# Score maxima by causal blocks of 32 queries and 4 heads, put into the query tile by DMA, and attention's steps in a new order

## The chip, the cores and the metric

The kernel runs on one core of a Trainium2 chip. The metric is the device time of one execution in microseconds (us). All times below are of that one core.

## What is computed

Two transformer-like layers on x of 16 x 256 x 128 (4096 tokens). Layer 0 has a modulated layer norm, causal attention, then a mixture of 8 experts (top 2) with a shared expert. Layer 1 is a gated recurrence with two gated products. The change is in the attention of layer 0, whose core is this (16 heads of 8 dimensions, 4 key heads, n = 256):

```python
q5 = q.reshape(b, reps, KV_HEADS, n, D_HEAD)
scores = jnp.einsum('brknd,bkmd->brknm', q5, k) / scale
causal = jnp.tril(jnp.ones((n, n), dtype=bool))
scores = jnp.where(causal, scores, jnp.float32(-jnp.inf))
p = jax.nn.softmax(scores, axis=-1)
s = jnp.einsum('brknm,bkmd->brknd', p, v)
```

## The kernel before

**Planning.** Python code plans the whole kernel ahead. `schedule()` makes jobs, each a short list of steps (a step has a name and a key such as the batch), and `arrange()` merges the jobs in the order that the string `ORDER1` spells (two characters pick the job whose next step comes) up to the first experts' tiles, and `ORDER2` for layer 1. The table `HELD` (how long a step holds its engine), `LANDS` and `BEHIND` (how long until its result can be used) serve only to choose PSUM banks and to place `fill` products, which keep TensorE active. Each engine then runs its own steps strictly in that order. A step waits on semaphores for what it needs.

**Stages.** First x is turned, normalised and modulated in chunks c of 512 tokens (8 chunks of 2 batches). Attention runs over 16 batches b, interleaved with the norms of later chunks and with the routing of earlier ones. After the last batch (`woh` 15, which writes X at L1400) SyncE fetches expert weights (`fetch`, `load_late`), the experts' tiles run, and then layer 1. From `woh` 15 on, memory of attention is used again, so nothing of the fetches can start sooner.

**Attention of one batch.** `spm`/`spe` (L977, L1808) put the queries of a chunk into QS, four groups g of 128 rows (4 key heads j x 32 rows: 24 of queries, 8 spare). `kzp`/`kza` make KZ, the keys with all rows but those of head j set to zero, and ones in rows 24 and 25. The softmax is shifted by a maximum, which rides in rows 24 and 25 of the queries as a high and a low part:

- `mxm` (L1001, TensorE): 12 products for each batch, 128 queries x 512 columns. For queries 0 to 127 the 512 columns are 4 heads x 128 keys; for queries 128 to 255 they are 2 heads x 256 keys.
- `mxr` (L1357, VectorE): `tensor_tensor_reduce` adds a causal mask CM and takes the maximum, 4 operations of 128 or 2 of 256 elements for each product, with a dummy output JK.
- `mh` (L1367 to L1370): rounds the maxima into a high part and a rest, in MP, a tile of 2 x 4 x 4 x 32 whose other columns are zero.
- `qmt` (L1010, TensorE): two steps of four 128x128 transposes of MP; `qma` (L1378, VectorE): QM = transposed MP + QS, two additions of 128x512.
- `atm` (L1024, L1026): scores again, keys as rows, from QM; 6 steps u of 2 products on 32 rows. `ate` (L1838, L1840): exponentials on ScalarE. `causal` (L2008): POOL sets what lies above the diagonal to zero.
- `pv` (L1039, L1041), `ot`, `nrt` (L1050), `nrd` (L1388), `stt` (L1058), `wom` (L1066), `woh` (L1396, L1400): weighted sum, division, output projection, residual.

PSUM has 8 banks: a ring RR of banks 0, 1, 6, 7 for everything, and a ring RE of two pairs (banks 2 to 5) for `atm`. QS, QM, KZ, PT0, PT1 and MX have two buffers each.

**SyncE** loads x, weights and masks, then issues 16 DMAs of 1 MB that set the experts' rows in DRAM to zero (L2103), one more (L2105), and the shared expert's weights (L2106, L2107). It then waits until 316 us. POOL's `scatter` (L2019) waits for all zero rows.

Of the kernel before, what the change touches and what calls it, by code (L numbers as in the profile page):

```python
# [7 lines left out]
F = mybir.dt.float32  # L8
R = mybir.dt.float32r
# [7 lines left out]
CH = 512  # L17
# [6 lines left out]
NS, LAG, NF, CAP, GB = 1, 3, 6, T, 6  # L24

# [15 lines left out]
NSEL = S_CAP + M2  # L41

# [5 lines left out]
def constants():  # L48
# [41 lines left out]
    "vm": ("PE", 0.81, None), "va": ("ACT", 0.157, None), "mxm": ("PE", 0.3, None), "mxr": ("DVE", 0.69, None),  # L90
    "mh": ("DVE", 0.4, None), "qmt": ("PE", 0.48, None), "qma": ("DVE", 0.6, None),
# [34 lines left out]
def cost(name, key):  # L126
    engine, held, table = HELD["t_" + name if key[:1] == ("t",) else name]
    if name == "mxr" and key[2] == 0:
        held = 0.845
    if name == "causal" and key[1] > 3:  # L130
        held = 1.19
    if name == "pv" and key[2]:
        held = 0.44
    return engine, held, table


def form_of(name, key):
# [10 lines left out]
    "BkBGBDAvAvAwAwBsB7B6BGBGBIChChCACACgCgCFCFBDBDBuBuAxAxBtBtCDCDB9B9B8B8BzBzBwBwBKBKBKCCCBCBCCB-B-BxBxBxByByBJBJBJCECECGCG"
    "AIAIB+B+B0BvBvBvB0BwB0ByCmBzCHCHAIAIBLBLBMBMCICiCiBdBdAICKCKAxAxCnBNCJCJBNAHAHCrBNBNCpCpCrAHB1B1B1BOBOCjCjCkCkBOBOCvCvAI"
    "BOBOCtCtCMCPCPDnDnDnDnCqCqCyCyCMCMB2B2B2CsCsCQCxCxCwCwCQDpDpCuCuCOCOCNCNCoCoBPBPCzCzC0CLCLB3B3DCCQCNDmDmB4B4C2C2C1C1DDDm"  # L150
    "DmCLCPCODqDqDrDrDHDHB5B5BPDsDsAIDKDKDFDFB5B5BRBRC7C7C7C4C4BPDEDEBPBPDLDLCRCRCRC8C8C8C5C5C5CSCSCSDoDoAJAJDNDNC6C6C3C3C3DI"
    "DICUCUAJAJCTCTDGDGBPAIAIAJC6DuC4AJDJDJClClCVCVDvAIDODODMDMDPDPDQC+C+C+CVCVD3D3D2D2BPC9C9C9DzDzCWCWBQBQDSDSCWCWDxDxCWD7D7"
    "DYDXDYDXEvEvCWEvEvBRBSD5D5D1D1EuDRDREuDtDtD0D0D4D4EuD6D6DWDWDVDVDwDyDwDyDAC-DUDTAJELD8CXC-DAD9CXD9D+D+EKDVETETENENEQEQDY"
    "DTDTDUDUDWEAD-D-ExExEWEWESESCXEAEEEEEuDXBREAEPEPEVEVDZDZDZEDEDEDECECEUEUEwEwDBDBCXEREREBE3DaDaDaDBDBEyEyEMEMBTE2BRECD-EE"
    "EBEBBUDbDbEXEXAJAJEOEODcDcEYEzEzE4E4E0E0EaEaAJDdE7EZDdDdDdEGEGEGDeDeEZE7CXF3F3F3F3BRE+E+DeDeDeCXCXAKAKE8CXE8EFEFEFAKFDFD"
    "AKAKAKEeEeEeEdEHEHEIEICZCZFBFBF5F5FCFCEgEdEdEgEgE-E-FAE9FAE9E6EbEbEbE5E5E6FEF6F6EcEfF7CYCYFTBVFSDeCZCaF7EcEfEfF8F8FFFFFX"
    "FXF2F2F2F2FfFfFVFVFUFUFHFHFIFIDfDfDfFcFcFGFGEJEJFeFeFbFYFYFMFMFZFZFbFJDhDhFaFaFJEcF4F4FWFWEJEJFdFdFgDfDfFKFLAKFKF-CZFMF+"
    "EiEiEiEhEhEhGJFhFhCbFKCZGJALFLALEjEjDfGGFiFiFkFjFjGGALGDGDDgDgALALAKAKGKGKAKE1E1GHGHFkGLEkEkGBGEGBGEGLElElGCGCGFGFFmFmFn"
    "FnElElF9F9GIGIGAGACcCZCdFlFoEmEmFHDhFJFLDiDhFmALGaFIFkFoGbDjGMG-GOEmEmDfG-DfGOG+FOFOFOG+G+G-EmFjEmFoG-G+FnGeGeGNGNGdGdGn"
    "GnFNGjGjGiGiFlFlGUFNFNGfGfHBALHBGUGkGkHCHCFQFQFPFPGSGTGTGTDhGSGSGlGlEnEnEnFRFRGmGhGhGcGcDkGPGQGQGPFpFpFpGRGRDhGPGQGRHAHA"  # L160
    "EnGmEnEnGgGgALALFqFqFqGoALEoEoEpEpHDHDHEGqGqIHIHHHFsFsHFHFHEFrFrFRFRDlEpHGGUGVGVIHGVHJHJFtFtIHGpGpHOHOFtFtHLHLGWGWGWHSHS"
    "FuGYGYGXGXFuFuFuEqEnEnHKHKGvGvGuFuFuEpGvHPHPIJIJHIHIIGIGHTHTGuGrGrGrHQHQGZGZHRHRGwGwHNIKIKHNHMHMGZGsGtGuHiHjGtGtIGGsErHU"
    "GZFvFvHWHWHVHVHmHmHoHoGwGsILILHnHnHbHbHbHvHkHkHvFvFvEpIGIMIMGxGxGxEsHZHZHZHaHaHqHqHpHtHtHpFvGyGyGyHcHcHcHaHrHrFxFxGzGzG0"
# [54 lines left out]


class Plan:  # L220
# [42 lines left out]
def arrange(P, jobs, done, order, banks=()):  # L263
# [3 lines left out]
    for n in range(0, len(order), 2):  # L267
# [6 lines left out]
        for m, (ring, *_) in enumerate(takes):  # L274
            k = ring.frees(done)[sum(r is ring for r, *_ in takes[:m])][2]
            ends = [(SIGNALS.get(s, s), wkey) for s, *wkey in ring.ends.get(k, ())]
            start = max([start] + [done[(s, *wkey)] + hop for s, wkey in ends if cost(s, wkey)[0] != engine])
# [33 lines left out]
    "kz_p": "kzp", "kz_a": "kza", "mx_mm": "mxm", "mx_red": "mxr", "mh": "mh", "qm_tp": "qmt", "qm": "qma",  # L311
# [16 lines left out]
def schedule():  # L328
# [3 lines left out]
    RR, RE = Ring([0, 1, 6, 7]), Ring(range(2))  # L332
# [59 lines left out]
    def copies(c, g):  # L392
        busy = [] if c < 2 or g == 4 else [("mxm", 2 * c - 3, g, u) for u in range(3)] + [("qma", 2 * c - 3, g // 2)]
# [14 lines left out]
    def maxima(b, g, u):  # L408
        yield stage("mxm", b, g, u, takes=[(RR, "mx", (b, g, u), ("mx_red", b, g, u))],
                    after=[("kzp", b), ("kza", b), ("spe", b // 2, g)] + ([("mh", b - 2)] if b > 1 else []))  # L410
        yield stage("mxr", b, g, u)

    def highest(b):
        yield stage("mh", b, after=[("mxr", b, g, u) for g in range(4) for u in range(3)] + ([("qmt", b - 1, h) for h in range(2)] if b else []))

    def shifted(b, h):
        yield stage("qmt", b, h, takes=[(RR, "qm", (b, h), ("qm", b, h))], after=[("mh", b)] + ([("atm", b - 2, u) for u in range(6)] if b > 1 else []))
        yield stage("qma", b, h)

    def attend(b, u):  # L420
        needs = [("qma", b, u // 2)] if u < 4 else [("qma", b, 0), ("qma", b, 1)]
# [5 lines left out]
        yield stage("atm", b, u, takes=[(RE, "at", (b, u), ("at_exp", b, u))], after=needs + busy)  # L427
# [14 lines left out]
    def residual(b):  # L442
# [3 lines left out]
        yield stage("woh", b)  # L446
# [1739 lines left out]
```

## Time and profile before

| | us |
|---|---|
| median of 3 runs | 721.96 |
| lowest, highest | 720.04, 722.82 |
| the profiled execution, span | 719.6 |
| end of the last X of attention | 316.3 |
| TensorE, VectorE, ScalarE, POOL busy | 663.8, 509.1, 477.8, 396.4 |

The span is from the first to the last instruction; the page gives no other time of this execution, so 719.6 stands for it, 2.4 us below the median. An engine's busy time is the union of its instructions' times. A TensorE record runs until its result has left the array, so records overlap, and its busy time is larger than the time that the array is taken. Idle time is put down to the engine that released the wait. The chain of waits counts each instant of the span once.

### The profile page before, as it was taken

How to read it: one execution, taken by the hardware profiler on the slowest of the kernel's cores; microseconds unless marked ns; L12 is line 12 of the kernel's file. 1: busy time of each engine (PE TensorE's matmuls, PEld its weight loads, DVE VectorE, ACT ScalarE, POOL GpSimd, SP SyncE). 2: the span in 40 equal slices, each digit the busy share in tenths (PEclk: the TensorE clock that was granted, in tenths of full speed). 3: DMA queues.
4: the chain of work that ended last, by engine and by line, in shares of the span. 5: the costliest groups of instructions: out<-in, count | busy, mean ns of one | idle time of the engine just before them, and what ended most of it. 6: DMA issues, size and time to landing. Idle time of an engine off the chain costs nothing.

```text
span 719.6 us, 12572 instructions
## 1 busy us (share of the span) xinstructions
PE 663.8 (92%) x3627; PEld 426.4 (59%) x3627; DVE 509.1 (71%) x1910; ACT 477.8 (66%) x743; POOL 396.4 (55%) x555
## 2 busy tenths in 40 slices
PE   7999999999899998889999799898879999999994
PEld 5544554545544544448889799875555665555542
DVE  6799899999989999865632454203557778786763
ACT  4767796868776877466444355543766899777663
POOL 5536464868777668533541355244565677744343
PEclk9999999999999999999999999999999999999998
DMA  9994000000000000027898588711101111000002
GB/s 252 379 383 162 1 1 1 16 16 15 27 5 24 12 19 23 15 72 232 252 273 242 170 239 249 217 33 31 30 25 28 30 30 37 23 15 1 15 1 73
DMA packets 65631, 66.01 MB, mean 92 GB/s; under 512 B 7121, under 2 KB 48554, under 8 KB 65562
## 3 DMA queue, kind: packets, MB, share of 16 engines
q1 hardware_dynamic: 59296, 52.12, 24.1%
q0 software_dynamic: 6208, 13.07, 5.6%
q8 instruction: 29, 0.48, 0.3%
q14 instruction: 40, 0.33, 0.1%
q10 hardware_dynamic: 58, 0.02, 0.0%
HBM read 37.33 MB, written 27.85 MB: 91 GB/s over the span
## 4 chain that ended last, share of the span: by engine, by line
PE 44%; DVE 27%; issue 9%; SPq 8%; POOL 4%; DMA 3%; ACT 3%; DVEq 0%; POOLq 0%; ACTq 0%
DVE JK L1357 10%; PE PS L1139 5%; PE PS L1119 3%; PE PS L1001 3%; PE PS L1039 3%; PE PS L944 3%; DVE XN L1642 2%; PE PS L950 2%; PE PS L1215 2%; POOL got L2047 2%; SPq L2132 2%; PE PS L956 1%; SPq L2130 1%; PE PS L1041 1%; POOL H L1978 1%
## 5 line engine op out<-in xcount | busy, mean ns | idle before, releaser
L1357 DVE CUSTOM_DVE_ANT_0 JK<-PS,CM 128x256 bf16<-128x256 f32 (+1 forms) x512 | 148.0, 350 | 5.6 <-PE PS L1001 5.0
L1877 ACT ACTIVATE GF<-PS,XN 128x256 f32<-128x256 f32 (+1 forms) x156 | 69.4, 455 | 65.3 <-PE PS L1119 35.3
L2047 POOL DMA_INDIRECT got<-expert_rows,IU x64 | 64.8, 1012 | 40.8 <-DMA got<-expert_rows,IU 21.4
L1001 PE MATMUL PS<-KZ,QS 128*128 128x512 f32 x192 | 83.6, 482 | 3.2 <-DVE QM L1378 1.4
L2019 POOL DMA_INDIRECT expert_rows<-five,IU x64 | 64.0, 1001 | 36.6 <-DMA expert_rows<-five,IU 14.2
L1139 PE MATMUL PS<-WD,GF 128*128 128x128 f32 x568 | 81.7, 275 | 0.0
L1139 PEld LDWEIGHTS PS<-WD,GF 128*128 128x128 f32 x568 | 73.8, 192 | 0.8
L1838 ACT ACTIVATE PA<-PS 128x1024 f32<-128x1024 f32 x64 | 63.9, 1025 | 13.9 <-PE PS L1024 12.8
L2008 POOL TENSOR_SCALAR_AFFINE_SELECT PA<-PA 128x256 f32<-128x256 f32 x128 | 49.2, 416 | 23.0 <-ACT PA L1838 22.6
L1978 POOL TENSOR_SCALAR H<-xc,MOD 128x256 f32<-128x256 f32 x56 | 33.7, 611 | 49.4 <-DVE xc L1321 49.2
L2032 POOL DMA_DIRECT2D expert_rows<-YT x39 | 21.6, 555 | 67.4 <-issue 43.9
L1001 PEld LDWEIGHTS PS<-KZ,QS 128*128 128x128 f32 x192 | 33.9, 188 | 39.4 <-DVE MX L1357 13.3
L1119 PE MATMUL PS<-XS,WU 128*128 128x256 f32 (+1 forms) x192 | 46.2, 352 | 1.4 <-DVE XS L1606 1.0
L2008 POOL TENSOR_SCALAR_AFFINE_SELECT PB<-PB 128x512 f32<-128x512 f32 x64 | 40.2, 653 | 9.5 <-ACT PB L1840 9.4
L1357 DVE DVE_READ_ACCUMULATOR2_ANT MX<- 128x1 f32 x512 | 41.2, 80 | 0.0
L1139 PEld LDWEIGHTS PS<-five,GF 128*128 128x128 f32 x256 | 33.6, 197 | 11.6 <-issue 9.4
L1642 DVE SCALAR_TENSOR_TENSOR XN<-got,W,XN 128x128 f32<-128x128 f32 x64 | 26.1, 468 | 20.1 <-DMA got<-expert_rows,IU 19.8
L1039 PE MATMUL PS<-PA,VA 128*32 128x512 f32 x256 | 34.6, 610 | 4.9 <-DVE SN L1388 1.8
L1631 DVE TENSOR_TENSOR YT<-PS,BD 128x256 f32<-128x256 f32 (+1 forms) x39 | 15.6, 400 | 33.0 <-PE PS L1139 33.0
L1847 ACT ACTIVATE OT<-PS 128x512 f32<-128x512 f32 x32 | 19.2, 599 | 27.5 <-PE PS L1041 27.2
L944 PE MATMUL PS<-X,CT 128*128 128x512 f32 x64 | 35.2, 633 | 1.8 <-DVE X L1713 1.3
L1139 PE MATMUL PS<-five,GF 128*128 128x128 f32 x256 | 34.4, 282 | 0.6 <-ACT rs L1767 0.6
(328 smaller groups left out, 1719.7 us busy)
## 6 DMA issues: line engine op xcount, KB each, us to landing
expert_rows<-five SPq DMA_DIRECT2D x16, 1024.0 KB, 13.4
WU<-in_L_ffn_up_w SPq DMA_DIRECT2D x39, 256.0 KB, 3.3
WD<-in_L_ffn_down_w SPq DMA_DIRECT2D x39, 256.0 KB, 3.5
XT<-expert_rows SPq DMA_DIRECT2D x32, 128.0 KB, 3.8
expert_rows<-YT POOLq DMA_DIRECT2D x32, 128.0 KB, 3.3
BD<-in_L_ffn_down_b SPq DMA_DIRECT2D x39, 64.0 KB, 3.4
PA<-in_L_attn_x SPq DMA_DIRECT2D x8, 256.0 KB, 5.2
out<-yo SPq DMA_DIRECT2D x8, 256.0 KB, 2.3
```

Of the source, the lines that this page charges most:

```text
L944: pe.matmul(bank("lc", c, s), centre, chunk(X, c), start=True, stop=True).then_inc(sems["cen"], 1)
L1001: pe.matmul(bk.rearrange("p (j n) -> p j n", n=wd), q, ks, start=True, stop=True).then_inc(sems["mx_mm"], 1)
L1039: m = pe.matmul(o, VA[:, 2 * b % 8, j, :], p0[:, j, 2 * h:2 * h + 2, :], start=True, stop=False)
L1119: pe.matmul(bk[:, 0:rows(u)], WU[u % NF][:, f], XS[slot["xs", u]][:, 0:rows(u)], start=True, stop=True).then_inc(sems["up"], 1)
L1139: m = pe.matmul(bk[:, b], g[:, b], wd[:, k, :], start=(k == 0 and t == 0), stop=(k == 3 and t == blocks - 1))
L1357: m = dve.tensor_tensor_reduce(JK[n % 2][:, s], bk[:, s], CM[:, 256 - wd:256] if wd == 128 else CM[:, 0:256], -1.0, 3.0e38, ALU.add, ALU.m ...
L1838: m = act.activation(PT0[b % 2][:, j:j + 2, g:g + 2, :].rearrange("p j g n -> p j (g n)"), two(both), ACT.Exp, scale=SCALE)
L1877: act.activation(GF[slot["gf", kind, u, k]][:, 0:n], bank("up", kind, u, k)[:, 0:n], ACT.Gelu, bias=bias).then_inc(sems["gelu"], 1)
L1978: m = pool.tensor_scalar(hb(b), xc[:, S * n:S * n + S], mod(l, kc, b), mod(l, ks, b), ALU.mult, ALU.add)
L2008: m = pool.affine_select(out=a, in_=a, pattern=[[0, 2 if u < 4 else 4], [1, 128]], compare_op=ALU.is_ge, fill=zero, base=0, channel_multip ...
L2019: pool.indirect_dma_start(out=XD[:, :], out_offset=bass.IndirectOffsetOnAxis(ap=IU[:, c, n, k:k + 1], axis=0), in_=HT[c % 2][:, k, :], in_ ...
L2047: pool.indirect_dma_start(out=got[b][n][:, k, :], out_offset=None, in_=XD[:, :], in_offset=bass.IndirectOffsetOnAxis(ap=IU[:, c, n, k:k + ...
```

## The change

1. **Maxima by causal blocks.** A product now has 32 queries x 4 groups as its 128 rows (block i of 8), and only the keys 0 to 32(i+1) of all 4 heads as columns: 128(i+1) columns, 4608 in a batch instead of 6144. A second product, in bf16 (CM), adds the causal mask to the last 32 keys of each head inside PSUM. Blocks 0 and 1 share a bank, 2 and 3 have one each, 4 to 7 take two neighbouring banks and two products each with a mask product each. In all 12 products and 12 mask products a batch.
2. **Plain reductions.** `mxr` is `tensor_reduce` (maximum, negated) straight from PSUM: 8 a batch, of 4 x 32(i+1) elements. JK goes.
3. **The shift goes into QS as rows.** `mh` is a copy (high part) and a subtraction (rest) into MH; `mxt` turns MH by one fp32r product with a unit matrix; `mxe` copies it to MT on ScalarE; `rowin` on SyncE issues 8 DMAs, each from 8 partitions of MT into one partition (4 KB) of QS. `qmt`, `qma`, QM and MP go. Every `atm` of a batch waits for all 8 DMAs.
4. **Buffers.** QS has 3 buffers, laid out 16 blocks x 4 groups x 32; all 8 PSUM banks are one ring, and `atm` and the wide maxima take a neighbouring pair.
5. **Zero rows.** The 16 DMAs of 1 MB are issued after the rows of batches 0 to 3, four after each.
6. **Order.** ORDER1 is new (1638 steps instead of 1813), ORDER2 is not. `route` and `plan_tiles` stand elsewhere, as everything does. From the decoded string, TensorE's steps between `mxt` and the first `atm` of the same batch are for batch 13: `mxm` 14,5, `ln_var`, `mxm` 14,6, `vm`; for batch 15: `atm` 14,1, `atm` 14,4, `pv` 13 (four steps), `stt` 12; for batch 0: `spm` twice, `ldt`, `vm`, `mxm` twice. Between `mxt` 0 and `mxt` 1 stand `atm` 0 (all six), three `mxm`, `pjm` and the steps named for batch 0.

The diff, cut to its core:

```diff
+NQ, ZB = 3, 4
+ROWIN = 16 * 8
+UNITS = ((0, 1), (2,), (3,), (4,), (5,), (6,), (7,))
...
+    "mh": ("DVE", 0.4, None), "mxt": ("PE", 0.12, None), "mxe": ("ACT", 0.2, None), "rowin": ("SP", 0.5, None),
...
+LANDS = {"wmod": 0.0, "rowin": 2.3, "zeros": 12.0, "fetch": 3.0, "store": 2.0, "load_late": 3.9}
...
-    RR, RE = Ring([0, 1, 6, 7]), Ring(range(2))
+    RR = Ring(range(8))
...
+            if u < 3:
+                at_ = 0
+                for i in UNITS[u]:
+                    m = scores(bank("mx", b, u)[:, at_:at_ + 128 * (i + 1)], i, QS[c % NQ][:, n0 + i].rearrange("p g n -> p (g n)"),
+                               kz[:, :, 0:32 * (i + 1)], i == UNITS[u][0], i == UNITS[u][-1])
+                    at_ += 128 * (i + 1)
+            else:
+                i, bk = UNITS[u][0], pair("mxw", b, u)
+                for n in range(2):
+                    m = scores(bk[:, n, 0:64 * (i + 1)], i, QS[c % NQ][:, n0 + i].rearrange("p g n -> p (g n)"),
+                               kz[:, 2 * n:2 * n + 2, 0:32 * (i + 1)], True, True)
+            m.then_inc(sems["mx_mm"], 1)
+
+        def scores(o, i, q, k, first, last):
+            o = o.rearrange("p (j n) -> p j n", n=32 * (i + 1))
+            js = k.shape[1]
+            pe.matmul(o, q, k, start=first, stop=False)
+            return pe.matmul(o[:, :, 32 * i:32 * i + 32], CM[:, 0:128], CM[:, 128:160].unsqueeze(1).to_broadcast([128, js, 32]),
+                             start=False, stop=last)
+
+        def mxt(b):
+            w.wait_ge(*at("mh", b))
+            w.wait_ge(*at("wq"))
+            for e in prior["mt", b]:
+                w.wait_ge(*at(*e))
+            pe.matmul(bank("mt", b)[:, 0:128], MH[b % 2][:, :, :, :].rearrange("p j k i -> p (j k i)"), UNIT[:, :], start=True, stop=True
+                      ).then_inc(sems["mt_mm"], 1)
 
         def atm(b, u):
-            w.for_all(each("qm", *((b, h) for h in ((u // 2,) if u < 4 else (0, 1)))))
+            w.wait_ge(rows_in[b % 2], ROWIN * (b // 2 + 1))
...
+            else:
+                i = UNITS[u][0]
+                wd = 32 * (i + 1)
+                m = dve.tensor_reduce(mt[:, :, i].rearrange("p (a j) -> p a j", a=2),
+                                      pair("mxw", b, u)[:, :, 0:2 * wd].rearrange("p a (j n) -> p a j n", j=2), AX.X, ALU.max, negate=True)
             m.then_inc(sems["mx_red"], 1)
...
+        def mxe(b):
+            w.wait_ge(*at("mt_mm", b))
+            if b > 1:
+                w.wait_ge(rows_in[b % 2], ROWIN * (b // 2))
+            act.activation(MT[b % 2][:, :], bank("mt", b)[:, 0:128], ACT.Copy).then_inc(sems["mt"], 1)
...
-        for n in range(16):
-            sp.dma_start(XD[2048 * n:2048 * n + 2048].rearrange("(p a r) d -> p a (r d)", a=4, r=4),
-                         ZT[:, :].unsqueeze(1).to_broadcast([128, 4, CH])).then_inc(zero_rows, 16)
...
+        def rowin(b):
+            n0 = 8 * (b % 2)
+            w.wait_ge(*at("mt", b))
+            for j in range(4):
+                for k in range(2):
+                    sp.dma_start(QS[b // 2 % NQ][32 * j + 24 + k:32 * j + 25 + k, n0:n0 + 8].rearrange("p i g n -> p (i g n)").bitcast(F),
+                                 MT[b % 2][32 * j + 8 * k:32 * j + 8 * k + 8, :]).then_inc(rows_in[b % 2], 16)
+            if b < ZB:
+                for n in range(16 // ZB * b, 16 // ZB * (b + 1)):
+                    sp.dma_start(XD[2048 * n:2048 * n + 2048].rearrange("(p a r) d -> p a (r d)", a=4, r=4),
+                                 ZT[:, :].unsqueeze(1).to_broadcast([128, 4, CH])).then_inc(zero_rows, 16)
```

## Rows read from the trace of the kernel before

**Rows 1.** The page, engines' busy time over the span.
```profile
PE 663.8 (92%) x3627; PEld 426.4 (59%) x3627; DVE 509.1 (71%) x1910; ACT 477.8 (66%) x743; POOL 396.4 (55%) x555
```

**Rows 2.** Windows: busy us and count by engine, granted clock, DMA share, GB/s.
```profile
20.00:60.00 40.00, 38.08 (x160) 18.57 (x158) 36.05 (x188) 30.27 (x49) 17.61 (x29) 1.00 1.03 379
...
100.00:140.00 40.00, 38.68 (x232) 19.69 (x234) 38.16 (x205) 31.23 (x46) 23.94 (x43) 1.00 0.01 4
```

**Rows 3.** The chain of waits by line, 60 to 300 us.
```profile
by line: DVE JK L1357 21.9%; PE PS L1001 9.8%; PE PS L1039 8.7%; issue 8.7%; PE PS L1041 3.7%; PE PS L1050 3.3%; PE PS L944 2.8%; PE PS L1010 2.7%; DVE QM L1378 2.6%; PE PS L1024 2.5%; PE PS L1066 2.2%; DVE MX L1357 2.1%; PE PS L950 2.0%; D
```

**Rows 4.** Timeline of VectorE, the first maximum and near 45 us: start, us, engine, line, operation.
```profile
31.81 0.42 DVE L1357 CUSTOM_DVE_ANT_0 JK<-PS,CM 128x256 bf16<-128x256 f32 x1 [0.30 <-PE PS L1001]
...
44.84 0.42 DVE L1357 CUSTOM_DVE_ANT_0 JK<-PS,CM 128x256 bf16<-128x256 f32 x1
...
45.19 0.28 DVE L1357 CUSTOM_DVE_ANT_0 JK<-PS,CM 128x128 bf16<-128x128 f32 x1
...
45.40 0.28 DVE L1357 CUSTOM_DVE_ANT_0 JK<-PS,CM 128x128 bf16<-128x128 f32 x1
```

**Rows 5.** Timeline of TensorE in the same stretch.
```profile
46.17 1.11 PE L1001 MATMUL PS<-KZ,QS 128*128 128x512 f32 x2 [0.34 <-DVE MX L1357]
```

**Rows 6.** The chain of waits at attention's end: start, us, what.
```profile
315.78 0.50 DVE X L1400
```

**Rows 7.** The chain of waits, pieces on TensorE at several places.
```profile
157.84 0.23 PE PS L1001
156.12 0.86 PE PS L950 x2
151.68 0.44 PE PS L1010 x4
158.07 0.99 PE PS L1039 x8
159.07 0.43 PE PS L1041 x8
313.96 0.79 PE PS L1074 x8
298.98 0.44 PE PS L1024 x3
```

**Rows 8.** Timeline of VectorE, the two additions of a batch.
```profile
54.42 1.27 DVE L1378 TENSOR_TENSOR QM<-PS,QS 128x512 fp32r<-128x512 f32 x2
```

**Rows 9.** Timeline of VectorE after attention, a plain reduction.
```profile
317.70 0.72 DVE L1577 TENSOR_REDUCE XN<-XN 128x68 f32<-128x544 f32 x1
```

**Rows 10.** Groups by shape, 20 to 300 us: count, busy us, mean ns, idle before.
```profile
L1838 ACT ACTIVATE PA<-PS 128x1024 f32<-128x1024 f32 x62 | 62.0, 1025 | 13.6 <-PE PS L1024 12.4 <-PE PS L1026 0.6
...
L1853 ACT ACTIVATE ST<-PS 128x256 f32<-128x256 f32 x14 | 5.4, 389 | 3.2 <-PE PS L1058 3.2
L1001 PEld LDWEIGHTS PS<-KZ,QS 128*128 128x128 f32 x192 | 33.9, 188 | 39.4 <-DVE MX L1357 13.3 <-issue 10.0 <-DVE QM L1378 5.1
```

**Rows 11.** Timeline of SyncE's queue, 0 to 60 us.
```profile
5.42 0.73 SPq L2090 DMA_DIRECT2D wqkv<-in_L_attn_w_q  x1
...
12.39 0.43 SPq L2097 DMA_DIRECT2D gate<-in_L_ffn_gate_w  x1
12.87 0.43 SPq L2098 DMA_DIRECT2D gbias<-in_L_ffn_bias  x1
...
14.29 35.60 SPq L2103 DMA_DIRECT2D expert_rows<-five  x16
```

**Rows 12.** DMA issues: count, KB each, median us from issue to landing.
```profile
XT<-expert_rows SPq DMA_DIRECT2D x32, 128.0 KB, 3.8
out<-yo SPq DMA_DIRECT2D x8, 256.0 KB, 2.3
five<-in_L_ffn_sw_up SPq DMA_DIRECT2D x1, 256.0 KB, 11.1
gate<-in_L_ffn_gate_w SPq DMA_DIRECT2D x1, 4.0 KB, 2.9
```

More of the change, by code:

```diff
@@ L148 @@
[L148 to L151, printed above, removed]
@@ L273, in arrange @@
         start = max([x[0], begun] + [done[(s, *k)] + hop for s, *k in after if cost(s, k)[0] != engine])
[L274 to L277, printed above, removed]
+        for m, (ring, what, *_) in enumerate(takes):
+            for k in ring.place(done, what in WIDE, sum(r is ring for r, *_ in takes[:m])):
+                ends = [(SIGNALS.get(s, s), wkey) for s, *wkey in ring.ends.get(k, ())]
+                start = max([start] + [done[(s, *wkey)] + hop for s, wkey in ends if cost(s, wkey)[0] != engine])
         waited = start > begun
@@ L392, in copies @@
     def copies(c, g):
-        busy = [] if c < 2 or g == 4 else [("mxm", 2 * c - 3, g, u) for u in range(3)] + [("qma", 2 * c - 3, g // 2)]
+        busy = [] if c < NQ or g == 4 else [("atm", b, u) for b in (2 * (c - NQ), 2 * (c - NQ) + 1) for u in range(6)]
         if g == 4 and c:
@@ L406, in keys, with maxima @@
         yield stage(name, b, after=[("spe", b // 2, 4)] + ([("atm", b - 2, u) for u in range(6)] if b > 1 else []))
[L408 to L411, printed above, removed]
+    def maxima(b, u):
+        yield stage("mxm", b, u, takes=[(RR, "mx" if u < 3 else "mxw", (b, u), ("mx_red", b, u))],
+                    after=[("kzp", b), ("kza", b)] + [("spe", b // 2, g) for g in range(4)] + ([("mh", b - 2)] if b > 1 else []))
+        yield stage("mxr", b, u)
     def highest(b):
[L414 to L418, printed above, removed]
+        yield stage("mh", b, after=[("mxr", b, u) for u in range(len(UNITS))] + ([("mxt", b - 2)] if b > 1 else []))
+        yield stage("mxt", b, takes=[(RR, "mt", (b,), ("mt", b))])
+        yield stage("mxe", b, after=[("rowin", b - 2)] if b > 1 else [])
+        yield stage("rowin", b)
     def attend(b, u):
-        needs = [("qma", b, u // 2)] if u < 4 else [("qma", b, 0), ("qma", b, 1)]
+        needs = [("rowin", b)]
         busy = [] if b < 2 else [("pv", b - 2, u // 2, 0)] if u < 4 else [("pv", b - 2, 0, 1), ("pv", b - 2, 1, 1)]
@@ L426, in attend @@
             busy = [("ldt", c) for c in range(NCH)]
-        yield stage("atm", b, u, takes=[(RE, "at", (b, u), ("at_exp", b, u))], after=needs + busy)
+        yield stage("atm", b, u, takes=[(RR, "at", (b, u), ("at_exp", b, u))], after=needs + busy)
         yield stage("ate", b, u)
@@ L445, in residual @@
         yield stage("wom", b, takes=[(RR, "wo", (b,), ("wo_h", b))])
-        yield stage("woh", b)
+        yield stage("woh", b, after=[("modg", 0)])
     def norm2(c):
@@ L538, in schedule @@
     over = [("woh", b) for b in range(NB)]
-    jobs += [(0.0, j) for j in (load_late(), plan(0), plan(1), turn_weights(), shared_units(RR, range(NS), over),
+    jobs += [(0.0, j) for j in (zeros(), load_late(), plan(0), plan(1), turn_weights(), shared_units(RR, range(NS), over),
                                 *(shared_out(c) for c in range(NS)), *(gelu("s", c) for c in range(NS)), *(fetches(n) for n in range(NF)))]
@@ L542, in schedule @@
         jobs += [(0.0, j) for j in (tile_rows(t), tile_up(t), gelu("t", t), tile_down(t))]
-    arrange(P, jobs, {(s, *key): 0.0 for s, *key in P.steps}, ORDER1, [(RR, lambda k: k), (RE, lambda k: 2 + 2 * k)])
+    arrange(P, jobs, {(s, *key): 0.0 for s, *key in P.steps}, ORDER1, [(RR, lambda k: k)])
     ends = dict(RR.ends)
-    for n in range(2):
-        ends[2 + 2 * n] = ends[3 + 2 * n] = RE.ends[n]
     RU, RD, RX = Ring(range(4), ends), Ring(range(4, 6), ends), Ring(range(6, 8), ends)
@@ L710, in program @@
     ld_w1, ld_sd = sem("ld_w1"), sem("ld_sd")
+    rows_in = [sem(f"rows_in{k}") for k in range(2)]
     stored = [sem(f"stored{k}") for k in range(2)]
@@ L724, in bank, with pair @@
         return PS[:, 512 * k:512 * k + 512]
+    def pair(*use):
+        k = slot[use]
+        return two(PS[:, 512 * k:512 * k + 1024])
     X = sb("X", [128, T])
@@ L759, in program @@
     xin = PT0[1][:, :, :, :].rearrange("p a b n -> p (a b n)").rearrange("p (a k d) -> p a k d", a=NCH, k=4)
-    CM = sb("CM", [128, 256], B16, part)
-    JK = [sb(f"JK{k}", [128, CH], B16, part) for k in range(2)]
+    CM = sb("CM", [128, 160], B16, part)
     cin = sb("cin", [16, 2, 128], where=part)
@@ L989, in vm, with mxm @@
             m.then_inc(sems["v_mm"], 1)
-        def mxm(b, g, u):
-            c, n0, bk = b // 2, S * (b % 2), bank("mx", b, g, u)
-            blk = 0 if u == 0 else 1
-            q = QS[c % 2][:, g, n0 + 128 * blk:n0 + 128 * blk + 128]
-            ks, wd = (KZ[b % 2][:, :, 0:128], 128) if u == 0 else (KZ[b % 2][:, 2 * u - 2:2 * u, :], 256)
-            w.wait_ge(*at("qs", c, g))
+        def mxm(b, u):
+            c, n0, kz = b // 2, 8 * (b % 2), KZ[b % 2]
+            w.for_all(each("qs", *((c, g) for g in range(4))))
```

204 lines of the change are left out of this document (102 added, 102 removed).

## The prediction

> **What bounds the kernel now.** The page comes first. It gives TensorE 92% of the span and VectorE 71% [rows 1], but a share over the span hides the stages. The windows separate them [rows 2]: in a stretch of attention VectorE is busy 38 of 40 us and TensorE 39, ScalarE 31, POOL 24. A TensorE record lasts longer than its turn in the array, so its busy time overstates it. The chain of waits shows the true order of things: between 60 and 300 us its largest line is the score maxima on VectorE (L1357, 21.9%, with 2.1% for reading the accumulator), then TensorE's lines [rows 3]. The timeline gives the reason. VectorE's reductions follow one another without a gap, 0.35 us from start to start for 256 elements and 0.21 us for 128 [rows 4], while TensorE's score products wait for a bank that VectorE has not emptied [rows 5]. So attention, which ends at 316.3 us with the write of X that lets SyncE begin to fetch experts [rows 6], is paced by VectorE, with TensorE close behind.
>
> How close: I price TensorE's attention steps by their shares of the chain and by starts in the timeline. A 512-column fp32r product is 0.23 us, a 512-column fp32 product 0.86, four transposes 0.44, eight products of a weighted sum 0.86 to 0.99 and of its second half 0.43, eight 8-column products 0.79, a pair of 32-row score products 0.22 [rows 7]. With the counts of ORDER1 up to the last `woh` this is maxima 44 us, weighted sums 42, fp32 products of normalisation and projection 47, splits 18, the shifted-query transposes (`qmt`) 14, the others 81: 246 us. Nineteen of these lie ahead of the first product for a maximum, at 31.5 us (VectorE waited 0.30 us for it and began at 31.81 [rows 4]). The stretch from there to 316.3 us is 285 us; 227 are work, some 21 are changes of tile form (ten groups in a batch, 0.1 to 0.2 each by the same starts). That leaves **37 us in which TensorE idles**, nearly all of it for VectorE.
>
> **The change part by part.**
> VectorE. Removed in each of 16 batches: 16 reductions of 256 and 16 of 128 elements, 16 x 0.35 + 16 x 0.21 = 9.0 us; two additions QM (1.27 for the pair) [rows 8]; of the three small steps at L1367 to L1370 one goes (0.2). Added: eight plain reductions over 4608 elements. Two rows price them: the old ones cost (0.35 - 0.21)/128 = 1.1 ns an element, and a plain reduction of 544 elements took 0.72 us in all [rows 9]. At 1.05 ns that is 4.8 us, and 0.08 to 0.15 a piece: 5.5 to 6.0. VectorE is 5 us a batch lighter, 80 us in all, and stops being the bound.
>
> TensorE. Twelve products of 512 columns (2.8 us at 0.23) become twelve of 4608 columns together (2.1 us) plus twelve mask products of 64 or 128 columns, each with its own weight load. The nearest row is a short product that is bound by its load, 0.1 us [rows 7], 1.2 us: together 3.3, +0.5 a batch. If the load costs the 188 ns of its record [rows 10], 24 loads are 4.5 us, +1.7 a batch, 27 us in all; this is the upper bound. Two `qmt` (0.88) become one 128-column fp32r product (0.1). Net -0.25 a batch, **-4 us**.
>
> ScalarE. One copy of 128x128 a batch: a copy of 256 columns takes 0.39 us [rows 10], I take 0.28 for half of it, 4.5 us in all on an engine with 9 us of 40 free [rows 2]: hidden. But it stands in ScalarE's order and can find an exponential of 1.02 us ahead of it [rows 10]. POOL: the memset is smaller, nothing else. QS in a third buffer and in runs of 32: same elements, no cost taken; cover is the idle time of ScalarE.
>
> SyncE and the DMAs, the new wait. What let the scores start was an addition on VectorE; now it is eight DMAs, and `atm` waits for all (128 counts). SyncE puts small ones out 0.47 us apart, also at 4 KB [rows 11]. Landing takes 2.3 us for the quickest here, 2.9 for a typical one [rows 12]. From the start of `mxt`: 0.3 product, 0.3 copy, 0.2 hand-offs, 7 x 0.47 = 3.3 issues, 2.3 landing: **6.4 us**. The code's own planner reckons 0.5 + 2.3 for the DMAs. TensorE works in order, and ORDER1 has put between `mxt` and the first `atm` of that batch only 2.7 to 5.6 us of work, 4.1 in the mean (batch 13: two maxima, `ln_var`, `vm`, 3.0; batch 15: two `atm`, two weighted sums, `stt`, 3.4); with changes of form 4.5. So it stands still 1.9 us a batch, 16 x 1.9 = **+30 us**, and behind `atm` wait every later product, then ScalarE's exponentials and POOL's masks. The bounds: landing under 2.3 us (no row) down to nothing issued in series, 3.1 us from `mxt`, no stall; to issues of 0.7 us as for `wqkv` [rows 11] and 3.8 us landing, 9.5 us, 5 a batch. The Trainium skill, "DMA: Bandwidth & Descriptors", in its anatomy of one DMA (GpSimd's path), gives a DMA a fixed cost of about 2.0 us and making descriptors only a small part of it. Taken for eight DMAs side by side, that would be the 3.1 us end and the sum of rival B.
>
> Zero rows. Sixteen 1 MB DMAs leave the front and follow the rows of batches 0 to 3, four each. Issued in a row they took SyncE 35.6 us, 2.2 apiece [rows 11]. Batches 0 and 1 are only 6.4 us of TensorE work apart. Batch 1's rows wait for four issues, 3.8 + 8.9 = 12.7 us after the copy of batch 0, then for their landing: ready 19 us after `mxt` 0 where 13 to 14 would do: **+5 us** once. Batches 2 and 3 come 12 and 16 us of work later, past the 11 us that 4 MB need at the 379 GB/s of the stretch that has them now [rows 2]. That a small load does wait behind zeros is in the trace: one of 256 KB landed after 11.1 us [rows 12]. The first scatter stands far behind the last zeros in the order: no cost.
>
> **The sum.** -37 (idle for VectorE) - 4 + 30 + 5 = -6 us. Waits on normalisation and masks that VectorE's load covers today come back, a quarter of the 37 by my estimate, 9 us, but POOL and ScalarE catch up while TensorE stands at `atm`; I count them as inside the 30. The profiled execution took 719.6 us, 2.4 below the median: 713.6 there, **716 us** as a median. From 316 us on nothing is changed and everything moves with it.
>
> **Rivals.**
> B: the rows are nearly free. If SyncE's eight issues overlap or land sooner, `mxt` to `atm` is about 4 us and covered. Then -37 - 4 + 9 (the waits no longer hidden) = -32 us: 690 us. For it: a row is only 4 KB, and the DMA engines' share is 0.01 in mid-attention [rows 2]. Against it: every run of small issues in the trace is 0.47 us apart [rows 11]. The rule of the Trainium skill, "DMA: Bandwidth & Descriptors", weighed above would give this time.
> C, slower: the row path takes longer than 6.4 us. Each us more costs 16; from 6.8 us the change ends slower. With issues of 0.51, landing 2.9 and 0.3 behind an exponential it is 7.6: +19 - 6 = +13, 735 us. For it: landings in the trace are mostly 2.5 to 3.8 us [rows 12], and ScalarE is in order. Against: those landings are of larger transfers, in stretches where the DMA engines have more to do than the 0.01 of mid-attention.
> D, slower: TensorE's loads bind. 24 weight loads a batch at 188 ns: +23 on my sum, +17: 739 us. Against: loads mostly hide behind the product before.
>
> **Chances.** My own case 0.35 (706 to 728), B 0.28, C 0.27, D 0.10. A measurement here tells 0.5%, 3.6 us. Faster by more: 0.21 of mine and all of B, 0.49. Within: 0.09 of mine and 0.04 of C, 0.13. Slower: 0.38. The range runs from B's 690 to D's 739.
>
> **What would show it.** The 16 x 9.0 = 144 us of maxima replaced by about 90 us of reductions, VectorE 27 of 40 busy in attention; TensorE's first `atm` product of each batch waiting for a DMA, 1.5 to 2.5 us each, about 30 in all, 7 in batch 1; issues 0.47 us apart; the last write of X near 310 us; the same 403 us after it. The forecast is wrong if `atm` hardly waits for DMAs (B), if it waits over 2.5 us a batch (C), or if the score products keep TensorE busy 4.5 us a batch (D).

## The result and the profile after

The changed kernel takes 767.9 us (median of 4 runs, 766.9 to 771.4) against 721.7 us of the kernel before: ratio 1.065, 95% interval 1.063 to 1.067. It is 46 us slower. The forecast was 716 us, 690 to 739.

The page of the changed kernel, busy time by engine, which answers [rows 1]:

```profile
span 764.9 us, 11748 instructions
PE 677.8 (89%) x3683; PEld 435.4 (57%) x3683; DVE 430.1 (56%) x967; ACT 479.8 (63%) x760; POOL 395.5 (52%) x556
PEclk9988898979777898879999999999999999999999
```

VectorE is 79 us lighter (509 to 430), as worked out. But the row of the granted clock has changed too: before, it stood at 9 (90% or more of full speed) in 39 of the 40 slices; now it is at 7 or 8 in 12 of the first 18 slices, which are mostly attention. The windows show both effects, beside [rows 2] (columns as there):

```profile
100.00:140.00 40.00, 33.98 (x186) 17.15 (x186) 22.56 (x48) 26.44 (x41) 20.09 (x35) 0.87 0.30 107
140.00:180.00 40.00, 35.31 (x208) 17.66 (x209) 21.08 (x51) 24.88 (x36) 20.16 (x36) 0.83 0.03 9
220.00:260.00 40.00, 33.56 (x173) 17.99 (x175) 21.72 (x48) 20.11 (x29) 22.91 (x36) 0.75 0.05 15
20.00:360.00 340.00, 290.80 (x1650) 152.31 (x1649) 193.98 (x454) 213.16 (x324) 186.47 (x312) 0.85 0.17 61
```

VectorE is busy 22 of 40 us instead of 38. TensorE, which was to gain from that, fell from 39 to 34 of 40, and its clock from 1.00 to 0.85 over attention. The clock has two levels, 2.4 and 1.2 GHz (granted 1.0 and 0.5), so a mean of 0.85 over 340 us is 102 us at half speed. Before the change there was one such stretch in attention, of 3.4 us. What TensorE waits for is new. The waits of the changed kernel, 20 to 370 us (total us, times, longest):

```profile
PE PS L1064 <- DMA QS<-MT: 33.1, 12, 4.2
PE PS L1067 <- DMA QS<-MT: 10.5, 4, 3.8
ACT PA L1878 <- PE PS L1064: 46.0, 24, 4.1
POOL PA L2050 <- ACT PA L1878: 68.0, 26, 8.1
```

In each of the 16 batches the first `atm` product stands still for the row DMAs, 43.6 us in all, 2.7 a batch; ScalarE waits behind TensorE, POOL behind ScalarE. The last write of X begins at 361.4 us instead of 315.8, 45.6 us later, and the span is 45.3 us longer: all of the loss is in attention.

The chain of waits across the first batch's rows shows how the wait is made (start, us, what):

```profile
38.67 0.15 PE PS L1051
38.85 0.29 ACT MT L1858
39.16 0.80 SPq L2153
40.01 0.65 SPq L2153
40.70 0.64 SPq L2153
...
43.42 0.64 SPq L2153
44.10 1.77 DMA QS<-MT
45.91 0.79 PE PS L1067
```

The product that turns the maxima (L1051), the copy (L1858), eight issues 0.70 us apart on SyncE, 1.8 us from the start of the last issue to the landing (the chain puts this issue, at 44.10, under the DMA): 7.4 us from the start of L1051, whose record begins at 38.51, to the data in the queries' tile. In the trace most batches take 7.1 to 7.5 us, batches 1 and 4 take 8.3 and batch 12 takes 8.0; the issues are 0.67 to 0.71 us apart in 14 of the 16 batches. The new reductions, by shape (count, busy us, mean ns):

```profile
L1403 DVE TENSOR_REDUCE MX<-PS 128x4 f32<-128x1024 f32 x16 | 19.5, 1220 | 16.2 <-PE PS L1043 16.0
L1397 DVE TENSOR_REDUCE MX<-PS 128x4 f32<-128x512 f32 x16 | 11.0, 688 | 15.0 <-PE PS L1043 14.8
```

All eight shapes together are 96 us busy, 6.0 a batch, and seven of the eight now wait for TensorE, where TensorE had waited for VectorE in [rows 5].

### The profile page after: what moved, and what is told of

Read it like the earlier page. It is cut to its first block, busy times and chain, and to the rows that moved or that the text cites. A ratio compares the mean times of both kernels' runs of the same rounds, so it can differ in the third digit from the quotient of the medians.

```text
span 764.9 us, 11748 instructions
## 1 busy us (share of the span) xinstructions
PE 677.8 (89%) x3683; PEld 435.4 (57%) x3683; DVE 430.1 (56%) x967; ACT 479.8 (63%) x760; POOL 395.5 (52%) x556
## 4 chain that ended last, share of the span: by engine, by line
PE 43%; SPq 21%; DVE 10%; issue 9%; DMA 7%; ACT 5%; POOL 4%; POOLq 0%; DVEq 0%; ACTq 0%
SPq L2153 10%; PE PS L1042 5%; DMA QS<-MT 4%; PE PS L1080 4%; PE PS L1064 3%; PE PS L1180 3%; PE PS L971 2%; PE PS L1256 2%; DVE XN L1678 2%; POOL got L2089 2%; SPq L2183 2%; SPq L2177 2%; SPq L2181 2%; SPq L2179 2%; PE PS L1082 2%
## 5 line engine op out<-in xcount | busy, mean ns | idle before, releaser
L1403 DVE TENSOR_REDUCE MX<-PS 128x4 f32<-128x1024 f32 (+3 forms) x64 | 64.2, 1020 | 46.5 <-PE PS L1043 46.1
L1180 PE MATMUL PS<-WD,GF 128*128 128x128 f32 x568 | 84.8, 278 | 1.0 <-ACT GF L1917 1.0
L1042 PE MATMUL PS<-KZ,QS 128*128 128x512 f32 (+5 forms) x192 | 79.3, 485 | 0.8 <-ACT KZ L1850 0.5
L1064 PE MATMUL PS<-QS,KZ 32*128 32x512 f32 x128 | 30.5, 625 | 33.1 <-DMA QS<-MT 33.1
L1042 PEld LDWEIGHTS PS<-KZ,QS 128*128 128x128 f32 x192 | 41.8, 218 | 21.0 <-issue 12.3
L1397 DVE TENSOR_REDUCE MX<-PS 128x4 f32<-128x512 f32 (+3 forms) x64 | 29.0, 484 | 30.3 <-PE PS L1043 30.0
L1043 PE MATMUL PS<-CM 128*128 128x64 bf16 (+1 forms) x192 | 43.2, 226 | 0.0
L1080 PE MATMUL PS<-PA,VA 128*32 128x512 f32 x256 | 42.6, 744 | 0.0
L1880 ACT ACTIVATE PB<-PS 128x1024 f32<-128x1024 f32 x32 | 32.4, 1026 | 15.4 <-PE PS L1067 14.4
L1064 PEld LDWEIGHTS PS<-QS,KZ 32*128 32x128 f32 x128 | 11.6, 230 | 51.7 <-DMA QS<-MT 36.4
```

Source lines behind the costliest of these rows:

```text
L1042: pe.matmul(o, q, k, start=first, stop=False)
L1064: m = pe.matmul(bk[:, n].rearrange("p (g i n) -> p g i n", g=2, i=8), kz[r, j, 0:128], q[r, n0:n0 + 8, u - u % 2:u - u % 2 + 2, :].rearran ...
L1080: m = pe.matmul(o, VA[:, 2 * b % 8, j, :], p0[:, j, 2 * h:2 * h + 2, :], start=True, stop=False)
L1180: m = pe.matmul(bk[:, b], g[:, b], wd[:, k, :], start=(k == 0 and t == 0), stop=(k == 3 and t == blocks - 1))
L1403: m = dve.tensor_reduce(mt[:, :, i].rearrange("p (a j) -> p a j", a=2), pair("mxw", b, u)[:, :, 0:2 * wd].rearrange("p a (j n) -> p a j n" ...
```

## The experiments

Theory W: the loss is TensorE's wait for the rows and the half clock that these pauses bring. Rivals: P, the new products (masks, more weight loads) make TensorE slower by themselves; S, the DMA traffic disturbs the engines.

**The rows go where nobody reads them.** SyncE issues the same 128 DMAs of the same size, but TensorE doesn't wait for them. (SyncE now waits itself for the rows of the batch before, an addition that this cut leaves out.)

```diff
-                    sp.dma_start(QS[b // 2 % NQ][32 * j + 24 + k:32 * j + 25 + k, n0:n0 + 8]...,
+                    sp.dma_start(QX[32 * j + 24 + k:32 * j + 25 + k, :].bitcast(F),
...
-            w.wait_ge(rows_in[b % 2], ROWIN * (b // 2 + 1))
```

> The eight row DMAs of a batch are issued as before but into a tile that nobody reads, and no score product waits for them; the softmax then runs without its shift, so that part of the computation is left out. Theory W (the loss is TensorE's wait for the rows, 44 us idle, and the half clock that these pauses bring, 102 us at half speed, up to 51 us of work): TensorE no longer waits for a DMA, the granted clock in attention goes back to about 0.98, and the time falls by 70 to 85 us, to 685 to 700 us. Rival P (the new products with their own weight loads and masks are what makes TensorE slower): only the 44 us of waiting go, 720 to 728 us, and the clock stays near 0.93. Rival S (DMA traffic itself disturbs the engines): no change beyond 10 us.

Measured: 708.7 us, ratio to the kernel before 0.979 (0.974 to 0.984). No wait for `QS<-MT` is left; its windows:

```profile
60.00:100.00 40.00, 38.71 (x246) 20.45 (x245) 28.41 (x67) 33.22 (x54) 23.77 (x46) 1.00 0.87 317
20.00:360.00 340.00, 320.64 (x2034) 191.95 (x2032) 223.47 (x524) 247.99 (x392) 210.11 (x338) 0.97 0.31 100
```

TensorE is back at 39 of 40 us, with a clock of 0.97 over the 340 us, 20 us at half speed. Against the changed kernel 59 us go. The wait was 44, which leaves some 16 more, if the waiting comes back us for us; that it does is assumed, not shown. (Counted to the last write of X, which begins at 300.9 us instead of 361.4, the gain is 60.5 us. What follows attention, which no edit touches, took 409.4 us in this execution and 403.5 in the changed kernel's, so some us of a difference between two profiled executions are not attention's.) S is out: the same DMAs run, the ones that set rows to zero at 317 GB/s beside them. P alone is out as well: by it the time had to stay at 720 us or more. But the 685 to 700 that W gave were not reached either.

**Working through the wait.** Ten dummy products before the wait of each batch's first `atm`, in its own bank.

```diff
+            if P.nth["atm", b, u] == 1 or b not in held:
+                held.add(b)
+                for _ in range(10):
+                    pe.matmul(bk[:, 0, 0:128], CT[:, C_RF:C_RF + 128], CT[:, C_RF + 128:C_RF + 256], start=True, stop=True)
             w.wait_ge(rows_in[b % 2], ROWIN * (b // 2 + 1))
```

> Ten dummy 128-column fp32 products (2.1 us at full clock) stand in front of the first score product of each batch, in the bank that this product will write, so that TensorE works through a part of its wait; nothing waits less. Theory W with the clock as its second part: granted clock from 0.93 to 0.97 or more, time 725 to 745 us. Rival (only the wait counts, the clock is a bystander because TensorE has slack): 768 us within 4. If the dummies lie on the path instead: 780 to 800 us.

Measured: 750.1 us (ratio 1.038, 1.035 to 1.041), 18 us under the changed kernel, though the rows come no sooner and TensorE has 160 more products (320 more records). Its window, and its largest wait for the rows:

```profile
20.00:360.00 340.00, 322.33 (x2081) 193.64 (x2079) 202.88 (x477) 228.27 (x347) 191.23 (x318) 0.95 0.20 70
PE PS L1068 <- DMA QS<-MT: 9.3, 7, 3.0
```

Half speed falls from 102 to 34 us. So 68 us less of it are worth 18 us, 0.26 us for each. That prices the clock by itself. By arithmetic an us at half clock costs half an us where TensorE alone paces; that only about half of this came back fits stretches in which other engines or waits set the pace, but which ones was not measured.

The same instruction at both levels, in the timeline of the changed kernel: the 512-column fp32 product with the mean took 2.08 us in a stretch at half clock (the window 205 to 213 us has 0.50) and 1.07 at full.

```profile
203.00:204.00 1.00, 0.00 (x0) 0.00 (x0) 0.00 (x0) 0.00 (x0) 1.00 (x3) 0.50 0.14 41
205.00:213.00 8.00, 8.00 (x26) 4.22 (x25) 3.62 (x9) 5.62 (x7) 2.97 (x7) 0.50 0.06 18
204.71 0.90 PE L1064 MATMUL PS<-QS,KZ 32*128 32x512 f32 x4 [3.41 <-DMA QS<-MT]
211.75 2.08 PE L983 MATMUL PS<-sq,CT 128*128 128x512 f32 x2
219.84 1.07 PE L977 MATMUL PS<-sq,CT 128*128 128x512 f32 x2
```

The clock falls inside TensorE's pause of 3.4 us, which ends at 204.7: it is still 1.00 in the window from 201 to 202 us and 0.50 from 203 to 204. The kernel before had its pauses too, the largest of 3.0 us, but not one in each batch.

**Fewer, larger DMAs.** Four of 16 partitions to 2, then two of 32 partitions to 4 (MH's order turned so that a part's 32 rows lie together).

```diff
-                for k in range(2):
-                    sp.dma_start(QS[b // 2 % NQ][32 * j + 24 + k:32 * j + 25 + k, n0:n0 + 8]..., MT[b % 2][32 * j + 8 * k:32 * j + 8 * k + 8, :])
+                sp.dma_start(QS[b // 2 % NQ][32 * j + 24:32 * j + 26, n0:n0 + 8]..., MT[b % 2][32 * j:32 * j + 16, :])
```

```diff
+            for k in range(2):
+                sp.dma_start(QS[b // 2 % NQ][24 + k:128:32, n0:n0 + 8]..., MT[b % 2][32 * k:32 * k + 32, :])
```

> Each batch's rows come by four DMAs (16 partitions to 2) instead of eight. Theory W: SyncE's issues shrink from 5.6 us to 2.8 us a batch, the rows land 2.8 us earlier, nearly all of the 2.7 us wait a batch goes and most of the half-clock time with it: 695 to 715 us. Rival P: at most the 44 us of waiting go, 725 us or more. If the landing and not the issuing is the cost (larger DMAs land later): 760 us or more.

> Two DMAs a batch (32 partitions to 4). Theory W: issues take 1.4 us, the rows are there about 4 us after the start of the turning product, which TensorE's work covers: 688 to 705 us, no more than 5 us of waiting for DMAs in all, clock 0.98. If the landing grows with the size of each DMA: no better than with four.

Measured: 720.3 us with four (ratio 0.996, 0.992 to 0.999) and 712.0 with two (0.985, 0.981 to 0.989). SyncE's queue with eight, four and two, from three timelines of the same batch:

```profile
73.82 5.46 SPq L2153 DMA_DIRECT2D QS<-MT  x8
```

```profile
71.48 2.71 SPq L2152 DMA_DIRECT2D QS<-MT  x4
```

```profile
67.73 1.24 SPq L2152 DMA_DIRECT2D QS<-MT  x2
```

The time of the issues falls with their number. The landing, from the start of the last issue, hardly grows with the size: it is 1.8, 1.9 and 1.9 us in most batches. From the start of the turning product to the data it takes some 7.2, 4.6 and 3.2 us. TensorE's waits for the rows go from 43.6 to 11.5 to 3.6 us. So what TensorE waited for was the issuing in series. The change with two DMAs is 56 us faster than with eight, and ahead of the kernel before.

**Is TensorE's new work the rest?** Two DMAs, without the twelve mask products; the shift is then the maximum with up to 31 later keys, which the softmax cancels.

```diff
-            pe.matmul(o, q, k, start=first, stop=False)
-            return pe.matmul(o[:, :, 32 * i:32 * i + 32], CM[:, 0:128], CM[:, 128:160]..., start=False, stop=last)
+            return pe.matmul(o, q, k, start=True, stop=True)
```

> On the version with two DMAs the twelve mask products of a batch are left out; the shift is then the maximum over the whole 32-key block on the diagonal, future keys included, which the softmax cancels, so the output stays what it was. Theory: with the rows out of the way TensorE paces attention, and a mask product costs 0.04 us to its start-to-start time and up to 0.1 with the load it exposes, 8 to 19 us over 16 batches: 695 to 705 us against 712. Rival (attention is now paced by the chain through ScalarE and POOL, TensorE has slack): 712 within 3.

Measured: 711.0 us, ratio 0.983 (0.977 to 0.989), the same as with the masks. The profiled execution had a clock of 0.961 over the span against 0.975. The other runs agree: 0.961 to 0.969 in the four without masks, 0.970 to 0.977 in the four with them. So without the mask products the clock is lower. Attention has 44 us at half clock against 24, and the 20 us more would cost 5 us at the 0.26 of the busy-wait run, an estimate. Time that the short products took may so have been given back as half clock. Why the clock is lower without them was not looked into.

**The zeros.** Four after batches 1 to 4 instead of 0 to 3.

```diff
-            if b < ZB:
-                for n in range(16 // ZB * b, 16 // ZB * (b + 1)):
+            if 1 <= b <= ZB:
+                for n in range(16 // ZB * (b - 1), 16 // ZB * b):
```

> On the version with two DMAs the four zero DMAs after batches 0 to 3 are moved to after batches 1 to 4, so that batch 1's rows have no zeros ahead of them. Theory: batch 1's wait of some 4 to 6 us and one half-clock stretch go, 705 to 708 us. Rival: the wait moves to batch 2 or is made up later, 712 within 2.

Measured: 708.2 us, ratio 0.982 (0.977 to 0.987), against 0.985 with the zeros early. The single wait for rows that the two-DMA version had, 3.6 us, is gone, and the median is 3.8 us lower; the intervals overlap. The wait was batch 1's: its rows took 7.7 us from the turning product, 6.4 of them from the last issue to the landing, behind batch 0's zeros, and 3.1 us once the zeros were moved.

**More dummy products**, and **the planner told the truth** (the latter with eight DMAs).

```diff
-..., LEAST, WORST, MOST, ... = ..., 0.6, 0.5, 2, ...
+..., LEAST, WORST, MOST, ... = ..., 0.8, 0.7, 3, ...
```

```diff
-    ... "rowin": ("SP", 0.5, None),
+    ... "rowin": ("SP", 5.5, None),
...
-LANDS = {..., "rowin": 2.3, ...}
+LANDS = {..., "rowin": 1.7, ...}
```

> On the version with two DMAs the planner places more dummy products (it tops up to 0.8 and 0.7 of its window instead of 0.6 and 0.5, up to 3 at a time). If what half clock is left in attention (24 us) costs much, it goes and the time falls to 702 to 708 us. If the dummies take TensorE's time on the path: 715 to 730 us.

> The changed kernel with eight DMAs, and only the planner's figures for the rows corrected to what the trace shows (5.5 us of issues and 1.7 us to landing instead of 0.5 and 2.3). The order is spelled out and stays; banks and dummy products follow the figures. Theory W: the waits stay, but dummy products now stand in them, so the half clock goes as in the busy-wait run: 735 to 752 us. If the order alone counts: 768 within 5.

Measured: 724.1 us (ratio 1.003, 1.000 to 1.005) and 763.8 us (1.059, 1.053 to 1.065). The profiled executions had a clock of 0.99 and 0.98. The first costs 12 us against the 712.0 of two DMAs, with 74 dummy products (148 records); the second is 4 us under the changed kernel's 767.9, with overlapping intervals, where the busy-wait run gained 18. In the second the planner put 187 dummy products (374 records) into attention, where the changed kernel had none:

```profile
L931 PE MATMUL PS<-CT 128*128 128x128 f32 x374 | 54.3, 291 | 0.0
PE PS L1064 <- DMA QS<-MT: 10.8, 11, 2.9
```

The waits shrank to 12.7 us and the products took their place. In these three runs dummies paid where each stood directly ahead of a wait that was there anyhow, as in the busy-wait run, and not where the planner spread them; that the others stood on TensorE's path is the likely reason, but was not traced product by product.

**What relieving VectorE is worth in the old kernel.** The kernel before, its maxima cut to a quarter of the keys.

```diff
-            for j in range(CH // wd):
-                m = dve.tensor_tensor_reduce(JK[n % 2][:, s], bk[:, s], CM[...], -1.0, 3.0e38, ALU.add, ALU.min, o[:, j:j + 1])
+            m = dve.tensor_reduce(o, bk.rearrange("p (j n) -> p j n", n=wd)[:, :, 0:wd // 4], AX.X, ALU.max, negate=True)
```

> The kernel before with VectorE's maxima cut to a plain reduction over the first quarter of each head's keys and without the mask (that part of the computation is cut; the softmax cancels any shift): 12 operations of 128 elements a batch, 0.3 us or less each, instead of 9.0 us. Everything else stays, the rows go through VectorE's addition. This prices what relieving VectorE alone is worth in the old order. My prediction's term (TensorE idles 37 us for VectorE, three quarters of it to be had): 690 to 697 us. Rival, from the run whose rows nobody reads (13 us gained where 32 were forecast): other waits step in and no more than 15 us are to be had, 706 to 715 us.

Measured: 707.7 us (median of three), ratio 0.979 (0.973 to 0.984): 15 us, inside the rival's range. (Its profiled execution is a fourth, with a longer span, 714.4 us, so only the pattern is read from it.)

```profile
60.00:100.00 40.00, 39.42 (x236) 22.32 (x233) 21.36 (x67) 32.52 (x49) 22.03 (x46) 1.00 0.06 18
DVE MX L1355 <- PE PS L1001: 50.8, 67, 2.9
```

VectorE's load falls to 21 of 40 us in this window (26 in the mean of 60 to 300 us) and VectorE now waits 51 us for the score products; TensorE stays at 39 of 40. TensorE had been about as close to being the bound as VectorE.

**Towards a version that beats both.** Two DMAs and late zeros, with one more step each, then with both.

> Two DMAs, zeros after batches 1 to 4, and no mask products. If TensorE's work paces attention: 8 to 19 us under the 708 of the same version with masks. If the earlier result holds (711.0 against 712.0: taking short products away lets TensorE pause and its clock fall instead): 705 to 710 us, clock lower than 0.98.

> Two DMAs, zeros after batches 1 to 4, and the planner's figures for the rows set to the two DMAs' (1.2 us of issues, 1.7 us to landing); only banks and dummy products follow. The figures hardly differ from the 0.5 and 2.3 it has: 708 within 3 by every theory; a larger move would show that the choice of banks matters.

> All that helped together: two DMAs, zeros after batches 1 to 4, the planner's figures of the two DMAs, no mask products. If the gains of the single runs add (704.5 without masks, 706.6 with the planner's figures, 708.2 without either): 701 to 704 us, ratio to the kernel before about 0.975. If they come out of the same waits: 704 to 707.

Measured: 704.5 us without masks (ratio 0.975, 0.970 to 0.980), 706.6 with the planner's figures for two DMAs (0.977, 0.973 to 0.981), 702.1 with both (0.972, 0.968 to 0.976; six runs). That is 19 us faster than the kernel before and 66 us faster than the change as it was made. The gains of the last two steps are inside their intervals one by one, so which of them counts how much can't be told.

## Why the prediction was wrong

**The sign.** The forecast was 6 us faster, the result 46 slower. The sum had four terms; in the runs they are these.

- *VectorE's relief, -37 and -4 us.* This step failed most: the idle time of TensorE that the relief could give back was put too high. (The quarter that was to come back was not in the sum; it was counted as inside the 30 us of waiting.) The run whose rows nobody reads has all of the change but the wait, and is 13 us faster than the kernel before, not 32 as rival B had it; relieving VectorE in the old kernel gave 15. The 37 us of idle TensorE were a difference of two large numbers, 285 us and a sum of prices taken from the tightest starts in the trace. Small surcharges at each product (a weight load not hidden, a change of form) would eat such a difference; that is an argument, not measured. Busy time, which I had set aside as overstated, was nearer to the truth: TensorE was busy 276.7 of the 295 us from 20 to 315 us, which leaves 18 us, half of the 37 (the row of the kernel before stands below this list, columns as in [rows 2]). And [rows 10] had put only 13.3 us of idle time ahead of the score products' weight loads down to VectorE's maxima, with 5.1 to its additions. Of the 41 us, 13 were to be had, a part of them possibly lost again to the 20 us at half clock of that run.
- *The wait for the rows, +30 us.* The mechanism was right and the size too small: 43.6 us. Issues were 0.70 us apart and not 0.47 as the loads in [rows 11] were; landing took 1.8 us and not 2.3. From `mxt` to the rows it was 7.4 us in batch 0, not 6.4, and the stall 2.7 a batch, not 1.9.
- *The clock, no term.* This step was missing, put at nothing without a reason. The prediction treated a stall as time lost once. A pause in every batch also brought TensorE down to half clock, 102 us of attention against 3. The busy-wait run prices 68 us of it at 18 us. The run without the wait agrees from the other side: 59 us gained for 43.6 us of waiting, 16 us more, with 82 us less at half clock, which at the busy-wait run's price would be 21.
- *The zeros, +5 us.* In the changed kernel batch 1's rows took 8.3 us instead of 7.4, and its stall was 4.2 us, 1.5 above the mean, which the 43.6 already hold. Four zeros took SyncE 4.2 us to issue and not 8.9, so they were out before batch 1's rows came. With two DMAs, where batch 1 comes sooner, moving the zeros gave 3.8 us.

So of the 52 us between the forecast -6 and the measured +46, about 28 are the relief, 9 the wait with the zeros and 16 the clock. That -13, 43.6 and 16 add up to the measured time proves nothing, since the 16 is the rest of the same three medians; the checks on it are the two runs that price the clock and the relief by themselves, 0.26 us for each us at half clock, and 15 us.

The window that the 276.7 us are from:

```profile
20.00:315.00 295.00, 276.66 (x1608) 144.75 (x1606) 271.30 (x1389) 215.87 (x316) 189.11 (x314) 0.99 0.18 66
```

**The rivals.** C was the nearest: the stall was over 2.5 us a batch, its sign of being right, and the 7.6 us from `mxt` to the rows are near the measured 7.4. That was luck in part, since its issues of 0.51 us were too quick and its landing of 2.9 us and the 0.3 us behind an exponential too long. Its 735 us had the same two errors in it, a relief that was too large and no clock. With both set right its stall of 49 us and the 5 for the zeros give 57 us slower, not 46, so it is above the measured stall by 10. B's mechanism (rows that cost nothing) is what two DMAs nearly reach, at 708 to 712 and not 690. D was wrong: the twelve pairs of product and mask start 0.21 to 0.36 us apart at full clock (200.48 to 200.75 for 320 columns and its mask), 3.6 us a batch where D had 4.5 and my own case 3.3, and taking the masks out gave 1 us with the zeros early (711.0 against 712.0) and 4 us twice with the zeros late (704.5 against 708.2, 702.1 against 706.6), each inside the intervals. Its sum had an error too: 24 loads at 188 ns are 1.2 us a batch more than my 3.3, 19 us and not 23, so D stood at 735 us, not 739.

**VectorE's prices** held: 6.0 us a batch of reductions, 5.5 to 6.0 forecast, and 22 of 40 us busy in the windows where 27 were forecast, since the batches also became longer.

**One fixed cost for eight DMAs.** The Trainium skill, "DMA: Bandwidth & Descriptors", in its anatomy of one DMA (GpSimd's path), gives a DMA a fixed cost of about 2.0 us. The trace agrees for the landing by itself, 1.8 us from the start of the last issue. Taken for eight side by side it would have given rival B, and that did not come: the seven gaps between the issues, 0.70 us each on SyncE's queue, were the larger part, 4.9 of 7.4 us.

**After attention** the forecast held for the changed kernel, 403.5 us against 403.8. The other runs had 403.4 to 409.4 us there, which the forecast didn't foresee and nothing here explains.

**What stays open.** That the clock accounts for the 16 us rests on two runs that roughly agree. Which surcharges keep TensorE from the 37 us was not measured one by one. The order alone (the new ORDER1 with the old maxima) was not tried, as the steps differ, and neither was the other cure for the wait, an order with more work between `mxt` and the first `atm`.

## What to carry to other kernels

Count a chain through DMAs by its issues: before the last of n small DMAs from one queue starts, n - 1 gaps between issues have passed (4.9 us here), and a plan that has 0.5 us for all the issues, as this kernel's had, doesn't see the reader's wait. A wait that an in-order TensorE meets in every round of a loop can cost more than its length, as the clock went down with the pauses here; look at the granted clock wherever an edit adds one. And don't bank the idle time of the second-busiest engine when it is a small difference of large sums: one run with the first engine's load cut shows what is really there.

## What the runs showed of the hardware that was not expected

- SyncE's issues of 4 KB from 8 partitions of SBUF into one took 0.63 to 0.65 us each, some 0.70 apart, where loads from DRAM of 4 KB took 0.43 us [rows 11]. From 16 partitions to 2 (8 KB) an issue took 0.61 us, and from 32 to 4 (16 KB) 0.52 us.
- The landing of such a DMA hardly grew from 4 KB to 16 KB, 1.8 us to 1.9 from the start of the issue. Behind four 1 MB DMAs on the same queue it took 6.4 us once (two DMAs, batch 1).
- 68 us at half clock cost 18 us of time, and 82 us some 16, less than the 34 and 41 that a TensorE without slack would lose.
- Raising the clock from 0.93 to 0.98 with 187 dummies spread by the planner gave 4 us (763.8 against 767.9): the dummies were 54 us of TensorE's busy time. Ten in front of each batch's wait gave 18.
